# First layer's edge loop: count items of 256 edges and 8 destinations, stores issued by ScalarE, destinations' loads by SyncE

## What is computed

```python
# L0: x is [6250, 64], 4 heads of 16
xl = (x @ W_l + b_l).reshape(n, HEADS, C)
xr = (x @ W_r + b_r).reshape(n, HEADS, C)
e = (edge_attr @ W_e).reshape(-1, HEADS, C)
g = leaky_relu(xl[src] + xr[dst] + e, 0.2)
logits = einsum('ehc,hc->eh', g, att)
ex = exp(logits - segment_max(logits, dst)[dst])
alpha = ex / segment_sum(ex, dst)[dst]
out = segment_sum(xl[src] * alpha[..., None], dst) + bias
# L1 (4 steps) and L3 (2 hops) sum over the edges alone:
neigh = segment_sum(emb[col], row)
```

## Time and profile before

| | |
|---|---|
| median of 3 runs | 6564.04 us (6562.2 to 6568.81) |
| the profiled execution's span | 6576.8 us |
| PE, DVE, ACT, POOL busy | 5007.3, 3022.6, 1799.8, 3882.2 us (76, 46, 27, 59%) |
| edge loop, first to last gather | 2411 us, 37% of the span |
| granted TensorE clock in the loop | 0.85 of full speed |

### The profile page before, as it was taken

The page is one execution under the profiler, slowest core; times in us unless marked ns, Lnnn a source line. Parts: engine busy times, 40 slices in busy tenths (PEclk is TensorE's granted clock), DMA queues, the critical chain, the costliest instruction groups (busy, mean ns, idle before and its releaser), DMA issues. The chain is left out here.

```text
span 6576.8 us, 115590 instructions
## 1 busy us (share of the span) xinstructions
PE 5007.3 (76%) x35178; PEld 4266.4 (65%) x35178; DVE 3022.6 (46%) x3931; ACT 1799.8 (27%) x3844; POOL 3882.2 (59%) x3427
## 2 busy tenths in 40 slices
PE   2338888888888888841999957877878787771898
PEld 2315665665566655531999957777777777771898
DVE  7757777777777777746322131111111111113322
ACT  0024555555555545510000012222222222220000
POOL 5748788888788888750000047777777777773000
PEclk9668888888888888955999955555555555555898
DMA  9335555555555555522999846666666666652895
GB/s 358 77 84 141 151 153 152 143 150 150 154 155 146 150 149 154 153 61 84 329 366 366 312 128 202 204 203 203 205 204 203 206 204 197 202 178 62 336 389 215
DMA packets 659138, 1262.13 MB, mean 192 GB/s; under 512 B 167881, under 2 KB 467466, under 8 KB 633268
## 3 DMA queue, kind: packets, MB, share of 16 engines
q1 hardware_dynamic: 381076, 726.95, 32.8%
q10 hardware_dynamic: 168480, 416.21, 18.9%
q0 software_dynamic: 109184, 115.05, 9.8%
HBM read 924.66 MB, written 490.51 MB: 215 GB/s over the span
## 5 line engine op out<-in xcount | busy, mean ns | idle before, releaser
L696 POOL DMA_INDIRECT att_gl<-tab_l,att_ix x1568 | 1933.5, 1233 | 487.6 <-issue 472.3
L1184 POOL DMA_INDIRECT sum_gl<-tab_l,sum_ixs x1568 | 1572.3, 1003 | 524.7 <-issue 477.8
L937 ACT ACTIVATE att_acc<-att_pc 128x392 bf16<-128x392 f32 x2352 | 1083.3, 497 | 1324.1 <-PE att_pc L715 1122.6
L712 PE MATMUL att_pc<-att_ohl,att_ohv 128*128 128x392 bf16 x2352 | 863.0, 367 | 272.0 <-DVE att_ohl L812 271.7
L1134 PE MATMUL sum_pm<-sum_msg,sum_S 128*128 128x64 f32 x3136 | 680.0, 407 | 425.6 <-ACT sum_msg L1158 425.5
L1134 PEld LDWEIGHTS sum_pm<-sum_msg,sum_S 128*128 128x128 f32 x3136 | 647.0, 314 | 465.7 <-issue 264.7
L715 PE MATMUL att_pc<-att_acc,att_ohv 128*128 128x392 bf16 x2352 | 855.7, 364 | 116.3 <-ACT att_acc L937 112.7
L1104 DVE TENSOR_TENSOR sum_t<-sum_pb,sum_gl 128x512 f32<-128x512 f32 x196 | 135.6, 692 | 1692.1 <-DMA sum_gl<-tab_l,sum_ixs 1692.1
L1116 PE MATMUL sum_pb<-sum_wbs,sum_ea 64*128 64x64 f32 x3136 | 694.5, 419 | 27.4 <-DMA sum_ea<-in_ea64T 27.4
L731 PEld LDWEIGHTS att_pl<-att_xe,att_S 128*128 128x128 f32 x3136 | 599.3, 216 | 159.8 <-issue 137.3
L1116 PEld LDWEIGHTS sum_pb<-sum_wbs,sum_ea 64*128 64x128 f32 x3136 | 676.1, 329 | 39.0 <-DMA sum_ea<-in_ea64T 27.6
(11 more groups left out here) (360 smaller groups left out, 5190.2 us busy)
## 6 DMA issues: line engine op xcount, KB each, us to landing
A<-att_acc SPq DMA_DIRECT2D x2352, 98.0 KB
l_a<-A SPq DMA_DIRECT2D x147, 1568.0 KB, 9.2
l_at<-AT SPq DMA_DIRECT2D x98, 1568.0 KB
att_dall<-in_dst ACTq DMA_DIRECT2D x224, 448.0 KB
sum_dall<-in_dst SPq DMA_DIRECT2D x196, 512.0 KB, 4.8
sum_a<-A SPq DMA_DIRECT2D x49, 1568.0 KB, 10.1
AT<-sum_at ACTq DMA_DIRECT2D x49, 1568.0 KB, 5.4
tot<-att_o ACTq DMA_DIRECT2D x56, 1022.0 KB
```

Source lines behind the costliest of these rows:

```text
L696: nc.gpsimd.indirect_dma_start(out=gl[s][:, c, :], out_offset=None, in_=g.tab_l, in_offset=bass.IndirectOffsetOnAxis(ap=ix[s][:, c:c + 1], ...
L712: nc.tensor.matmul(pc[c][m % 2][:, 0:LO], ohv[c][h][:, m, :, 0], ohl[c][h][:, m // 2, :, m % 2], start=True, stop=False)
L937: nc.scalar.activation(acc[c][n % CR][:, :], pc[c][m % 2][:, 0:LO], ACT.Copy).then_inc(s_acc[c], 1)
L1184: nc.gpsimd.indirect_dma_start(out=gl[q][:, j, :], out_offset=None, in_=g.tab_l, in_offset=bass.IndirectOffsetOnAxis(ap=ixs[q][:, j:j + 1] ...
```

## The change

Two neighbouring chunks are counted as one item: an item has up to 256 edges of one window of 8 destinations. It has two one-hot row matrices and the carry matrix interleaved (`ohv` with three 16-bit values side by side in place of two) and two column one-hots (`ohl`), and three matmuls in place of two. There are 784 + 783 = 1567 items, in two chains of 784; a turn has `TI` = 28 items per chain, `SLOTS` = (4, 4, 4, 2, 4, 4, 4, 2), and `acc` has 4 buffers per chain. The items' rows are gathered in pairs of chunks (`IT` = 13). The store of an item is issued by ACT, after the copies of the next item of both chains; the load of `dall` is issued by SP.

```diff
-CI = 1176
-CJ = 6
-CB = 7
-SLOTS = (6, 6, 6, 4, 6, 6, 4, 4)
-CR = 7
+CI = 784
+TI = 28
+MP = 6
+SLOTS = (4, 4, 4, 2, 4, 4, 4, 2)
+WS = max(SLOTS)
+CR = 4
...
-        for k, w in (("d", NT), ("k", IT)):
+        for k, w, q in (("d", NT, CQ), ("k", IT, CQ // 2)):
...
             def _(sp):
+                def load_dst(n, k):
+                    c0 = n * GQ
+                    if not known(n, NQ):
+                        sp.wait_ge(s_S, n + (1 - NQ))
+                    sp.dma_start(dall[k][:, :, :].rearrange("p g e -> p (g e)"),
+                                 g.d["dst"][bass.ds(c0 * P, GQ * P)].partition_broadcast(P)).then_inc(s_dall[k], 16)
...
-                    nc.tensor.matmul(pc[c][m % 2][:, 0:LO], ohv[c][h][:, m, :, 0], ohl[c][h][:, m // 2, :, m % 2],
-                                     start=True, stop=False)
+                    for k in range(2):
+                        nc.tensor.matmul(pc[c][m % 2][:, 0:LO], ohv[c][h][:, m, :, k], ohl[c][h][:, m, :, k],
+                                         start=k == 0, stop=False)
...
-                    v.tensor_tensor(ohv[c][h][:, 0:w, :, :], spread(c_row2[:, :, :].unsqueeze(1), [P, w, P, 2]),
-                                    spread(g.vals[:, bass.ds(n0, w), :].unsqueeze(2), [P, w, P, 2]), ALU.is_equal)\
+                    v.tensor_tensor(ohv[c][h][:, 0:w, :, :], spread(c_row3[:, :, :].unsqueeze(1), [P, w, P, 3]),
+                                    spread(g.vals[:, bass.ds(n0, w), :].unsqueeze(2), [P, w, P, 3]), ALU.is_equal)\
...
-                    v.tensor_tensor(ohl[c][h][:, 0:w // 2, :, :], spread(c_lo2[:, :, :].unsqueeze(1), [P, w // 2, LO, 2]),
-                                    spread(g.lo[:, bass.ds(n0, w)].rearrange("p (j two) -> p j two", two=2).unsqueeze(2),
-                                           [P, w // 2, LO, 2]), ALU.is_equal).then_inc(s_oh[c], 1)
+                    v.tensor_tensor(ohl[c][h][:, 0:w, :, :], spread(c_lo2[:, :, :].unsqueeze(1), [P, w, LO, 2]),
+                                    spread(g.lo[:, bass.ds(n0, w), :].unsqueeze(2), [P, w, LO, 2]), ALU.is_equal)\
+                        .then_inc(s_oh[c], 1)
...
+                def store(i, c, n):
+                    row = act.value_load(g.flush[0:1, bass.ds(i * (TI) + (c * CI + n), 1)])
+                    act.wait_ge(s_acc[c], i * (TI) + (n + 1))
+                    act.dma_start(g.A[bass.ds(row, P), :], acc[c][n % CR][:, :],
+                                  bounds_check="skip_entire_dma").then_inc(s_st[c][n % CR], 16)
...
                                 for c in range(CH):
                                     count(i, t, c, place.index(m))
+                                for c in range(CH):
+                                    n = at0[t] + place.index(m)
+                                    if not (n == 0 and known(i, 1)):
+                                        store(i, c, n - 1)
```

More of the change, by code:

```diff
@@ L643, in edge_loop @@
         o = [st.sb(f"o{s}", [P, GB, W0 + HEADS]) for s in range(R)]
-        ohv = [[st.sb(f"ohv{c}_{h}", [P, CJ, P, 2], BF16) for h in range(2)] for c in range(CH)]
-        ohl = [[st.sb(f"ohl{c}_{h}", [P, CJ // 2, LO, 2], BF16) for h in range(2)] for c in range(CH)]
+        ohv = [[st.sb(f"ohv{c}_{h}", [P, WS, P, 3], BF16) for h in range(2)] for c in range(CH)]
+        ohl = [[st.sb(f"ohl{c}_{h}", [P, WS, LO, 2], BF16) for h in range(2)] for c in range(CH)]
         pl = [st.ps(f"pl{k}", [P, 512]) for k in range(2)]
@@ L671, in _ @@
             def _(sp):
-                def turn(i):
[L673 to L683, removed]
+                def load_dst(n, k):
[4 more added lines that the diff above has]
+                                 g.d["dst"][bass.ds(c0 * P, GQ * P)].partition_broadcast(P)).then_inc(s_dall[k], 16)
+                def turn(i):
+                    for t in range(SL):
+                        load_dst(i * SL + t, t % NQ)
+                repeat(sp, TURNS, turn)
             @block.gpsimd
@@ L763, in turn @@
                         place = PLACE[SLOTS[t]]
-                        for m in range(CJ):
+                        for m in range(MP):
                             if m in place:
@@ L951, in turn @@
                         first, second = not known(b, 1), not known(b, 2)
-                        if not (final and t + 3 >= SL):
-                            load_dst(i * SL + (t + 3), (k + 3) % NQ)
                         place = PLACE[SLOTS[t]]
-                        for m in range(CJ):
+                        for m in range(MP):
                             if m in place:
@@ L974, in _ @@
                 turns(act, TURNS, turn)
+                for c in range(CH):
+                    store(TURNS - 1, c, TI - 1)
                 keep_sums(LAST - 1, 0, 2)
@@ L982, in _ @@
                     act.wait_ge(s_out[s], 16 * TURNS)
+                for c in range(CH):
+                    for b in range(CR):
+                        act.wait_ge(s_st[c][b], 16 * (CI // CR))
         old = st.sb("old", [P, LO], BF16)
@@ L1538, in item_columns @@
     with Stage(nc, "itemc") as st:
[L1539 to L1541 removed]
+        hi = st.sb("hi", [P, IT, 2 * P])
+        rkr = st.sb("rkr", [P, IT, 2 * P])
+        lor = st.sb("lor", [P, IT, 2 * P])
+        groups = [(h, r) for h in range(2) for r in range(0, IT, 4)]
         pt = [st.ps(f"pt{k}", [P, 4, P]) for k in range(2)]
@@ L1582, in _ @@
                 step(v.tensor_scalar(near[:, :], near[:, :], g.dcol1[:, :], -1.0, ALU.mult, ALU.add))
-                step(v.tensor_copy(g.vals[:, :, 1], near[:, 0:NI]))
+                step(v.tensor_copy(g.vals[:, :, 2], near[:, 0:NI]))
                 dve.sem_inc(s_e, 1)
@@ L2114, in lay_out @@
     a["dst_rows"] = rows
-    srow = np.full((NCH + 1, P), PAD, np.int32)
-    srow[:NCH] = src.reshape(NCH, P)
-    a["src_rows"] = srow
+    pairs = np.full((2, NPR + 1, 2 * P), PAD, np.int32)
+    pairs[0, NPR] = NP + 1
+    pairs[0, :NPR], pairs[1, :NPR] = dst.reshape(NPR, 2 * P), src.reshape(NPR, 2 * P)
+    a["dst_pairs"], a["src_pairs"] = pairs[0], pairs[1]
     for n, k in ((16, "ea16T"), (64, "ea64T")):
```

99 lines of the change are left out of this document (46 added, 53 removed).

## The result

The changed kernel takes 6835.3 us (median of 4 runs, 6820.5 to 6843.7); the kernel before, run beside it, 6566.4. The ratio is 1.0405 [1.0393, 1.0418]: **269 us slower**, where +154 was forecast.

What follows compares the result with a forecast made beforehand. POOL's gathers, issued without pause, were taken to bound the loop: +160 us for gathers held by longer one-hots, -6 ahead of the loop, other work hidden, 6564 + 154 = 6718 us; range 6655 to 6840.

Steps and rivals of the forecast that it cites:

- The bound and the mechanism: Edge loop: POOL's gathers set the pace and wait for DVE's two-input operations; longer ohl adds 160 us.
- strictly in step: Edge loop: each ohv and ohl pair lengthens exactly one gather, by 1.32 us for 336 pairs after the change.
- the 545 and 380 us of today's one-hots: DVE in the loop: present sums of ohl (545 us) and ohv (380 us), from which the change was costed.
- DVE's term: One-hots in the loop: ohl's sum on DVE rises by 163 us, DVE busy 2024 us, fitting under POOL.
- The upper bound 6777: Whole time: the forecast's own upper bound, from 213 us more in the gathers.
- ohv again 0.953: Row one-hots on DVE: 1536 values still take 0.953 us with three values side by side.
- Rival B: ohv on DVE runs at one value per cycle, 1.76 us; DVE becomes the bound, 6763 us; chance 0.13.
- Hidden while POOL sets the pace: Stores on ACT: a pair takes 1.4 us, and ACT's 2229 us of work fit the 2571 us loop.
- Rival C: ACT in the loop becomes the bound through its stores, at 0.80 us each, 6821 us; chance 0.12.
- both of its signs: For ACT as bound: POOL would wait for messages, and the copies' idle time would end with issue.
- Ahead of the loop: Preparation: six fewer gathers save 7.5 us, histogram 1, items' columns and rows add 3; together -6 us.

Runs made afterwards that it cites:

- e7: Changed kernel with ohv in even inner runs of 6, stores back on SP and destinations' loads on ACT: 6698 us, ratio 1.0184.
- e4: Kernel before with the even steps' ohl one pair of items wider (added columns unused) and six store buffers for seven: 6642.3 us, ratio 1.0097.
- e5: Kernel before with each ohl cut into operations of two items: 6474.5 us, ratio 0.9832.
- e1: Changed kernel with stores back on SP and destinations' loads on ACT: 6815.5 us, ratio 1.0372.
- e6: Changed kernel with each ohl cut into operations of two items: 6848.3 us, ratio 1.0411.
- e8: Changed kernel with ohv in inner runs of 6, stores on SP, destinations' loads on ACT, and ohl cut into operations of two items: ratio 0.9922.
- e9: Changed kernel with stores on SP, destinations' loads on ACT, and ohl cut into operations of two items; ohv keeps inner runs of 3: ratio 1.0085.
- e12: Kernel before with ohl and ohv cut into operations of two items and S into 512 and 384 values: 6551.6 us, ratio 0.9969.

## Why the prediction was right in sign and short by 115 us

- **The bound and the mechanism**: right. e7 is nearest to the forecast's world: ohl longer, ohv even, the roles as before, with the rest of the change in it. DVE's busy time rose by 157 us (2017.7), its longest gather is 2.278 us (2.27 forecast). Its stretch is 2550.1 - 2411.3 = 139 us longer and its gathers' sum 2072.4 - 1933.5 = 139, for +160 forecast (bounds 107 and 213); in the measured time 0.0184, 121 us, for +154. A gather ended 0.82 us after the ohl it met, in both kernels. That gathers and pairs go strictly in step was too much: in e4 two thirds of the added ohl time reached them, and in the step of the changed kernel shown above two pairs held three gathers, for 0.94, 0.45 and 1.58 us (the forecast had that each pair costs exactly one gather). e4 (gathers +62 us) and e5 (-170) show that an operation with two SBUF inputs holds the gathers. The Trainium skill ("SBUF — State Buffer", Who interferes with whom) states that a VectorE instruction with two SBUF inputs contends with a GpSimd one that reads SBUF, and these runs agree; its inference that tensor_tensor doesn't stall descriptor generation they contradict.
- **Small slips in the sums**: the 545 and 380 us of today's one-hots are those of a window with 278 of 280 pairs; for the loop they are 548 and 382, so DVE's term should have been +160 for +163. The upper bound 6777 leaves out the -6 that the lower one has. Neither changes the outcome.
- **"ohv again 0.953"**: the step that failed first. It was costed by the count of values, and the shape had changed under the count. 1.218 us; DVE +105 (336 x 0.268 + 112 x 0.131), and as gathers go in step with DVE, the gathers' sum from e7 to e1 rose by as much, 106. Rival B's price of 1.76 was too high, but its sentence that anything between the two rates would lengthen pairs and gathers as well is what happened; it was left out of the sum. The Trainium skill ("Vector Engine (DVE) Microarchitecture Reference", 5.1 Performance modes) says that with two sources a pair of values may span two rows of odd length; taken as a reason for an unchanged duration, the trace disagrees, 1218 against 951 ns. The same page (5.2 Measured stream behaviour on trn2) has pairs of 4-byte words that start on an odd word, on both sources, at 1.30 ns a column where contiguous ones take 1.054. Whether that is the cause here no run shows.
- **"Hidden while POOL sets the pace"**: the second step that failed. The store was sized rightly (1.26 us a pair for 1.4), and the sum of ACT's work fitted the stretch as said. But a busy sum is no cover: copies wait behind stores, PE's matmuls and sums behind copies, S and the messages behind those. Alone it is worth 22 us or less here, since POOL's own bound lies almost as high; with the gathers freed it is worth 214 to 252. Rival C had the place but the wrong test, ACT's busy sum against POOL; both of its signs came, POOL's waits for messages and copies whose idle time ends with issue.
- **Ahead of the loop**: -6 forecast, +2.2 measured. The memset that follows the 13 destinations' gathers came 8.6 us earlier (-7.5 forecast):

```profile
195.91 5.32 POOL L245 MEMSET tab_hT<- 1x6272 f32 x1 [3.15 <-POOLq L226]
```

  (204.53 in the kernel before.) The items' columns gave it back: they began 8.1 us earlier (365.38 for 373.45) and their last operation at the same time (416.58 for 416.57), so they took 8 us more, where +3 was forecast. And the first gather waited 12.36 us for its indices, for 9.78 before. The first gather of kernels with the same head began between 428.0 and 434.7, so these few us can't be split further.
- **The sum**: 121 (ohl) + 124 (odd ohv, SP storing) + 22 (roles) = 267 of 269. That it adds up is no proof, since each term is the step from one of four runs to the next (before, e7, e1, changed), and the first holds all of the change that isn't ohv's inner run or the roles. The split between the last two depends on the order in which they are undone: 72 and 74 the other way round.
- **The chances**: the forecast's mechanism held, and B and C, at 0.13 and 0.12 as rivals, both came in part and in addition to it, neither as priced. That 6835 is inside the range is luck: its upper end was made from either rival alone and at full size, and their parts together with the forecast happened to stay 5 us below it.

The best kernel here is the one before with ohl (and S) cut: 0.9825 [0.9802, 0.9848], some 115 us faster, and not to be told apart from the one with ohl alone cut (0.9832).

## What to carry over

When a POOL DMA queue is the bound, look at the longest DVE operation with two SBUF inputs, not at DVE's busy time: cutting it in two or three cost 0.04 to 0.06 us of DVE's time a cut here and gave back 1.7% on the kernel before, and nothing on the changed kernel, where another bound stood just behind. Cost a reshaped operation by its inner run and not by its count alone, and when work moves to another engine's queue, ask what is queued behind it and who waits for that, even where its busy sum fits. Undo suspected causes in pairs: undone one at a time, two bounds of nearly equal height each look small.

## What the runs showed of the hardware that was not expected

- A DVE tensor_tensor on 16-bit values with inner runs of 3 took 0.69 ns a value, with runs of 2 or 6 0.52 (1218 and 951 ns for 1536 values).
- Only the operation under way holds a gather, not those queued behind it. In e5, DVE and POOL:

```profile
1511.84 0.95 DVE L809 TENSOR_TENSOR att_ohv<-att_c_row,cnt_vals 128x1536 bf16<-128x1536 f16 x1
1512.71 1.51 DVE L814 TENSOR_TENSOR att_ohl<-att_c_lo,cnt_lo 128x784 bf16<-128x784 f16 x3
```
```profile
1512.10 1.52 POOL L696 DMA_INDIRECT att_gl<-tab_l,att_ix  x1 [0.30 <-issue]
1513.92 1.12 POOL L696 DMA_INDIRECT att_gl<-tab_l,att_ix  x1 [0.30 <-issue]
```

  The gather that began in ohv ended at 1513.62, 0.83 us after ohv's end at 1512.79, with three ohl operations back to back behind it.
- An operation of 784 values takes 0.56 us in the rows, but three back to back take 1.51: each begins before the one ahead has ended. A cut's price is the 0.04 to 0.06 us by which DVE's busy time rose per cut (e5, e6, e8, e9 and e12, each against the run without these cuts), not the fixed 0.15 of an operation.
